# Turning the distance factors on VectorE and through memory, and a new order of joins, masks and gathers, in a graph layer on one core

## What is computed

```python
h  = relu(bn1(conv1(x)));  x_conv = relu(bn2(conv2_17taps(h)) + x)
s  = x @ w_se.T + b_se                    # three numbers for each node
dist = sq[:, None] + sq[None, :] - 2 * s @ s.T
A  = exp(-dist) * mask
x_nmp = A @ relu(x @ w_msg.T + b_msg)
gi = [x_conv, x_nmp] @ w_ih.T + b_ih;  gh = x @ w_hh.T + b_hh
r, z = sigmoid(gi_r + gh_r), sigmoid(gi_z + gh_z)
out = x0 + (1 - z) * tanh(gi_n + r * gh_n) + z * x
```

## Time and profile before

| | us |
|---|---|
| median of 3 runs (287.84 to 287.97) | 287.91 |
| the profiled execution | 288.4 |
| its span | 286.5 |
| TensorE busy (matmuls) | 276.6 (97%) |
| VectorE busy | 243.0 (85%) |
| ScalarE busy | 164.5 (57%) |
| GpSimd busy | 62.5 (22%) |

### The profile page before, as it was taken

The page is one execution under the profiler, slowest core; times in us unless marked ns, Lnnn a source line. Parts: engine busy times, 40 slices in busy tenths (PEclk is TensorE's granted clock), DMA queues, the critical chain, the costliest instruction groups (busy, mean ns, idle before and its releaser), DMA issues.

```text
span 286.5 us, 5279 instructions
## 1 busy us (share of the span) xinstructions
PE 276.6 (97%) x1866; PEld 249.3 (87%) x1866; DVE 243.0 (85%) x551; ACT 164.5 (57%) x271; POOL 62.5 (22%) x124
## 2 busy tenths in 40 slices
PE   7899899999999999999999999999999999999993
PEld 6598886999888998899889998899988998899993
DVE  5998988978998889968998789969998787976565
ACT  3786468745565277545665267564674366561363
POOL 6500020831116102430026102340026100250000
PEclk9999999999999999999999999999999999999999
DMA  7600044566252512654153532645021540023002
GB/s 236 251 3 0 0 150 146 151 182 184 75 174 72 128 70 74 222 68 155 42 176 86 86 130 74 220 47 176 2 84 65 76 146 3 0 37 39 0 2 73
DMA packets 9373, 27.99 MB, mean 98 GB/s; under 512 B 2706, under 2 KB 3220, under 8 KB 8468
## 3 DMA queue, kind: packets, MB, share of 16 engines
q1 hardware_dynamic: 7184, 23.98, 24.0%
q0 software_dynamic: 2016, 3.67, 9.5%
q10 hardware_dynamic: 148, 0.01, 0.0%
HBM read 23.41 MB, written 7.91 MB: 109 GB/s over the span
## 4 chain that ended last, share of the span: by engine, by line
PE 67%; DVE 17%; issue 6%; ACT 5%; POOL 2%; DMA 1%; SPq 0%; DVEq 0%; ACTq 0%; POOLq 0%
PE ps L1194 20%; PE ps L1196 19%; PE ps L1195 19%; PE ps L1278 4%; PE ps L1244 3%; DVE stats L754 2%; DVE wt_lo L796 2%; DMA xin<-x_first 1%; ACT wt_hi L455 1%; POOL rstd L378 1%; PE ps L1255 1%; DVE aff L952 1%; DVE v_lo L877 1%; DVE y L897 1%; PE ps L1268 1%
## 5 line engine op out<-in xcount | busy, mean ns | idle before, releaser
L1194 PE MATMUL ps<-v_hi,wt_hi 128*128 128x256 f32 x320 | 92.6, 289 | 2.6 <-DVE v_lo L865 1.4
L1196 PE MATMUL ps<-v_hi,wt_lo 128*128 128x256 f32 x320 | 90.1, 282 | 0.0
L1195 PE MATMUL ps<-v_lo,wt_hi 128*128 128x256 f32 x320 | 89.9, 281 | 0.0
L1194 PEld LDWEIGHTS ps<-v_hi,wt_hi 128*128 128x128 f32 x320 | 60.3, 188 | 4.7 <-DVE wt_lo L796 1.8
L1195 PEld LDWEIGHTS ps<-v_lo,wt_hi 128*128 128x128 f32 x320 | 60.3, 188 | 0.3
L1196 PEld LDWEIGHTS ps<-v_hi,wt_lo 128*128 128x128 f32 x320 | 60.2, 188 | 0.0
L384 POOL TENSOR_TENSOR scale<-vpe,neg_half 128x8 f32<-128x8 f32 x6 | 10.6, 1768 | 87.8 <-DVE scale L771 87.8
L1194 PE MATMUL ps<-h_hi,wt_hi 128*128 128x512 f32 (+1 forms) x67 | 26.2, 391 | 0.2 <-ACT gate L612 0.2
L1196 PE MATMUL ps<-h_hi,wt_lo 128*128 128x512 f32 (+1 forms) x67 | 25.8, 386 | 0.0
L1195 PE MATMUL ps<-h_lo,wt_hi 128*128 128x512 f32 (+1 forms) x67 | 25.7, 383 | 0.0
L607 ACT ACTIVATE gate<-ps,par 128x512 f32<-128x512 f32 x14 | 9.6, 687 | 20.6 <-PE ps L1196 20.6
(11 more groups left out here) (160 smaller groups left out, 621.5 us busy)
## 6 DMA issues: line engine op xcount, KB each, us to landing
w<-ln_rows SPq DMA_DIRECT2D x6, 1024.0 KB, 4.7
mask<-adj_t SPq DMA_DIRECT2D x8, 512.0 KB, 3.5
out<-x_t SPq DMA_DIRECT2D x7, 512.0 KB, 5.1
out<-gate POOLq DMA_DIRECT2D x14, 256.0 KB, 4.1
xin<-x_nm SPq DMA_DIRECT2D x6, 512.0 KB, 3.3
xt<-x_t SPq DMA_DIRECT2D x6, 512.0 KB, 5.7
w<-w_conv SPq DMA_DIRECT2D x1, 576.0 KB, 5.9
gate<-w_gate SPq DMA_DIRECT2D x1, 576.0 KB, 6.9
```

Source lines behind the costliest of these rows:

```text
L1194: pe.matmul(dst, wt_hi[:, blk, :], hi, start=start, stop=False)
L1195: pe.matmul(dst, wt_hi[:, blk, :], lo, start=False, stop=False)
L1196: return pe.matmul(dst, wt_lo[:, blk, :], hi, start=False, stop=stop)
```

## The change

It touches groups 2 to 7 (`g > BY_TRANSPOSE`, with `BY_TRANSPOSE = 1`); groups 0 and 1 stay.

- `factor_transposes` and `factor_rows` go. VectorE makes one `transpose` of 128 by 256 numbers (`turn`) at the head of its group; it works in blocks of 32x32.
- SyncE stores the result with four DMAs (runs of 32 numbers, 128 bytes; 1024 of them in all), waits, and loads it back with two DMAs (480 runs of 512 bytes) into `rows`. This stands at the head of SyncE's group, ahead of the load of `xts`.
- `distance` moves from behind sub-convolution 2 of 9 to behind the seventh; both gathers move to behind the ninth.
- ScalarE: `exponent` moves behind `m_shared(g, 2)` and behind `h_high` and `graphs_of` of the next group; then come `xc_high`, `ghn_rows(g, 0)`, `n_high` twice.
- VectorE: the masks move from ahead of `ln_apply` to behind `add_shared(g, 1)`, ahead of the last joins and `ln_stats`; `n_low` twice moves behind `xc_low`.
- TensorE: in gates 0, the products of `xc` come ahead of those of the messages.

The diff, cut to its core:

```diff
+            def factor_loads(g):
+                done = g - 1 - BY_TRANSPOSE
+                sp.wait_ge(turned_ready, done + 1)
+
+                upto(sp, rows_landed, 32 * done)
+                for i in range(4):
+                    ns = slice(32 * i, 32 * i + 32)
+                    sp.dma_start(slot_rows.rearrange("(i s) q n -> s q i n", s=SLOT)[:, :, :, ns],
+                                 turned[ns].bitcast(F32).rearrange("s (q i) n -> s q i n", q=2)).then_inc(turned_stored, 16)
+                sp.wait_ge(turned_stored, 64 * (done + 1))
+
+                sp.wait_ge(dist_ps, g)
+                sp.dma_start(rows[:, 0:4:2, :].bitcast(F32), slot_rows).then_inc(rows_landed, 16)
+                sp.dma_start(rows[0:P - KD, 1:4:2, :].bitcast(F32), slot_rows[KD:P]).then_inc(rows_landed, 16)
...
+                if g > BY_TRANSPOSE:
+                    factor_loads(g)
...
                 else:
-                    factor_rows(g)
-                    m_shared(g, 0)
...
+                    m_shared(g, 1)
+                    if ahead:
+                        h_high(g + 1, 0)
+                        h_high(g + 1, 1)
+                        graphs_of(g + 1, 0)
+                        graphs_of(g + 1, 1)
+                    m_shared(g, 2)
+                    exponent(g)
+                if g > BY_TRANSPOSE:
+                    xc_high(g)
+                    ghn_rows(g, 0)
+                    n_high(g, 0, 5)
+                    n_high(g, 1, 7)
...
+            def turn(g):
+                done = g - 1 - BY_TRANSPOSE
+                dve.wait_ge(slots_ready, g + 1)
+
+                upto(dve, turned_stored, 64 * done)
+                dve.transpose(turned[:].bitcast(F32).rearrange("p b (k s) -> p b k s", k=2),
+                              slots[:, :, :, 0:KD].bitcast(F32).rearrange("p k b s -> p b k s")).then_inc(turned_ready, 1)
...
+                    turn(g)
                     update(g - 1, 1)
                     join_b(g, 0)
                     join_b(g, 1)
                     add_h(g)
-                masked(g, 0)
-                masked(g, 1)
...
+                else:
+                    if ahead:
+                        h_low(g + 1, 1)
+                    add_shared(g, 1)
+                    masked(g, 0)
+                    masked(g, 1)
+                    join_y(g, 1, 0)
+                    join_y(g, 1, 1)
+                    if g + 2 < NG:
+                        ln_stats(g + 2)
                 xc_low(g, 0)
                 xc_low(g, 1)
+                if g > BY_TRANSPOSE:
+                    n_low(g, 0, 5)
+                    n_low(g, 1, 7)
...
             def gates_xc(g, c):
                 xc = (xc_hi[:, cols(c)], xc_lo[:, cols(c)])
                 pe.wait_ge(xc_lo_ready, NCH * g + c + 1)
+                if n_last(g, c):
+                    three(bank(4), IH(R, 0), *xc, False, False)
+
+                    pe.wait_ge(n_lo_ready, NCH * g + 1)
+                    three(bank(5), IH(N, 0), *xc, True, False)
+                    three(bank(6), IH(Z, 0), *xc, False, False)
+                    return
...
                 sub_conv(g, 0)
-                if g > 1:
-                    factor_transposes(g)
                 sub_conv(g, 1)
-                if g > 1:
-                    distance(g)
                 sub_conv(g, 2)
...
                 sub_conv(g, 6)
-                gather(g, 1, 7)
+                if g <= BY_TRANSPOSE:
+                    gather(g, 1, 7)
+                else:
+                    distance(g)
                 sub_conv(g, 7)
                 sub_conv(g, 8)
+                if g > BY_TRANSPOSE:
+                    gather(g, 0, 5)
+                    gather(g, 1, 7)
                 gates_h(g, 0, ahead)
                 if ahead:
                     conv1(g + 1, 0, 0)
                     conv1(g + 1, 1, 7)
-                gates_n(g, 0)
-                gates_xc(g, 0)
+                if g <= BY_TRANSPOSE:
+                    gates_n(g, 0)
+                    gates_xc(g, 0)
+                else:
+                    gates_xc(g, 0)
+                    gates_n(g, 0)
```

More of the change, by code:

```diff
@@ L58, with gnn_kernel @@
 NPAR = 14
-def gnn_kernel(nc, x_first, x_nm, x_t, adj_t, w_in, w_conv, w_gate, par_in, row_in, bias_in, ln_rows, out):
+def gnn_kernel(nc, x_first, x_nm, x_t, adj_t, w_in, w_conv, w_gate, par_in, row_in, bias_in, ln_rows, slot_rows, out):
     ctx = ExitStack()
@@ L115, in gnn_kernel @@
         slots = sb("slots", [P, 2, GB, SLOT], F32R)
+        turned = sb("turned", [P, GB, SLOT], F32R)
         rows = sb("rows", [P, 4, P], F32R)
@@ L179, in gnn_kernel @@
             sem("rows_ready"))
+        turned_ready, turned_stored, rows_landed = sem("turned_ready"), sem("turned_stored"), sem("rows_landed")
         dist_ps, e_ready, a_ready, nmp_ps, n_hi_ready, n_lo_ready = (
@@ L190, in gnn_kernel @@
             sem("zd_ready"), sem("out_ready"))
+        BY_TRANSPOSE = 1
         BY_MATMUL = 1
@@ L249, in distances @@
             engine.wait_ge(s_ready, 2 * g + 2)
-            upto(engine, rows_ps, g)
+            if g <= BY_TRANSPOSE + 1:
+                upto(engine, rows_ps, g)
+            else:
+                engine.wait_ge(turned_ready, g - 1 - BY_TRANSPOSE)
             left, right = slots[:, 0], slots[:, 1]
@@ L704, in _ @@
                 candidate(g - 1, 1)
-                if g == 1:
-                    m_shared(g, 0)
+                m_shared(g, 0)
+                if g <= BY_TRANSPOSE:
                     factor_rows(g)
-                else:
-                    factor_rows(g)
[L710 to L723, removed]
+                    exponent(g)
[9 more added lines that the diff above has]
+                    n_high(g, 1, 7)
+                else:
+                    m_shared(g, 1)
+                    if ahead:
+                        h_high(g + 1, 0)
+                        h_high(g + 1, 1)
+                        graphs_of(g + 1, 0)
+                        graphs_of(g + 1, 1)
+                    m_shared(g, 2)
+                    exponent(g)
+                if g > BY_TRANSPOSE:
+                    xc_high(g)
+                    ghn_rows(g, 0)
+                    n_high(g, 0, 5)
+                    n_high(g, 1, 7)
+                else:
+                    ghn_rows(g, 0)
+                    xc_high(g)
                 if ahead:
@@ L1142, in _ @@
                 join_y(g, 0, 1)
-                n_low(g, 0, 5)
+                if g <= BY_TRANSPOSE:
+                    n_low(g, 0, 5)
                 if ahead:
                     h_low(g + 1, 0)
[L1146 to L1153, removed]
+                if g <= BY_TRANSPOSE:
+                    add_shared(g, 1)
+                    n_low(g, 1, 7)
+                    join_y(g, 1, 0)
+                    if ahead:
+                        h_low(g + 1, 1)
[3 more added lines that the diff above has]
+                else:
+                    if ahead:
+                        h_low(g + 1, 1)
+                    add_shared(g, 1)
+                    masked(g, 0)
+                    masked(g, 1)
+                    join_y(g, 1, 0)
+                    join_y(g, 1, 1)
+                    if g + 2 < NG:
+                        ln_stats(g + 2)
                 xc_low(g, 0)
                 xc_low(g, 1)
+                if g > BY_TRANSPOSE:
+                    n_low(g, 0, 5)
+                    n_low(g, 1, 7)
                 if g + 2 < NG:
@@ L1258, in distance @@
             def distance(g):
-                pe.wait_ge(rows_ready, g + 1)
+                if g <= BY_TRANSPOSE:
+                    pe.wait_ge(rows_ready, g + 1)
+                else:
+                    pe.wait_ge(rows_landed, 32 * (g - BY_TRANSPOSE))
                 if g == 0:
@@ L1327, in gates_h, with n_last @@
                 three(bank(6), HH(Z), *h, True, False)
+            def n_last(g, c):
+                return c == 0 and g > BY_TRANSPOSE
             def gates_n(g, c):
+                last = n_last(g, c)
                 nm = [n[:, c * HALF:(c + 1) * HALF, :] for n in (n_hi, n_lo)]
@@ L1334, in gates_n @@
                         pe.wait_ge(wt_lo_ready, LOT_OF_GATES)
+                if last:
+                    three(bank(4), IH(R, 1), *nm, False, True).then_inc(r_ps, 1)
+                    three(bank(5), IH(N, 1), *nm, False, True).then_inc(gin_ps, 1)
+                    three(bank(6), IH(Z, 1), *nm, False, True).then_inc(z_ps, 1)
+                    return
                 three(bank(4), IH(R, 1), *nm, False, False)
@@ L1444, in _ @@
                 sub_conv(g, 5)
-                gather(g, 0, 5)
+                if g <= BY_TRANSPOSE:
+                    gather(g, 0, 5)
                 sub_conv(g, 6)
-                gather(g, 1, 7)
+                if g <= BY_TRANSPOSE:
+                    gather(g, 1, 7)
+                else:
+                    distance(g)
                 sub_conv(g, 7)
                 sub_conv(g, 8)
+                if g > BY_TRANSPOSE:
```

(5 more changed lines are left out.)

## The result

| | before | after |
|---|---|---|
| median of 6 runs, us | 287.94 (287.84 to 288.01) | 289.93 (289.48 to 292.64) |
| ratio to before | | 1.0083 (95%: 1.0065 to 1.0102) |
| the profiled execution, us | 288.4 | 289.6 |
| its span, us | 286.5 | 287.7 |

The kernel became 0.8% slower; 288.5 had been forecast, 0.2% slower (0.58 us, where the medians differ by 1.99). Before, six runs lie within 0.2 us; after, they spread over 3.2. So there are two things to find: what holds the fastest runs 1.64 us above the fastest of before (289.48 against 287.84), and what adds up to 3 us to others.

A forecast was written before the change was run, and what follows sets the result against it. TensorE's own work was taken to bound the kernel. Savings of 3.12 and 0.55 against waits of 4.10 and 0.15 gave +0.58 us: 287.91 + 0.58 = 288.5 us, range 286.9 to 290.8.

The forecast's parts named there:

- the wait at the second half of convolution 1: TensorE waits for n_low before writing bank 7: 0.77 us in groups 2 to 6, 0.25 more in group 2; 4.10 together.
- two chains: Ahead of n_low: ScalarE's list with ghn_rows before n_high, and VectorE's own work, free at G + 2.1; either alone holds it.
- G: Start of the first matmul of gates_h(g, 0), forecast at T + 16.5; convolution 1's second half due at G + 2.79.
- the rivals: TensorE never waits, 284.2 us, chance 0.09; rows late, 294.5 if 1 us late, 0.07; masks late, 290, 0.12.
- What TensorE saves: TensorE's list in groups 2 to 7: transposes 0.44 and one return less 0.08, 0.52 us a group, 3.12 in all.
- one break less: TensorE's gathers put together make one return less, saving 0.08 us a group in groups 2 to 7.
- The wait for the slots: In group 2, TensorE's slot transposes wait for GpSimd's last write of the slots; removing them saves another 0.55 us.
- Group 7: No convolution 1 there; a wait for n_low(0) behind the third matmul of gates_xc costs 0.15 us.
- The way through memory: Turned slots stored and reloaded by SyncE: rows at T + 7.0 to T + 11.9, hidden with 3 us to spare.
- T: The start of group 4, at 154.05, from which the prediction counts; TensorE asks for the rows at T + 11.4.
- The rival of late rows: At distance behind sub-convolution 7, TensorE waits for rows in each of six groups; 1 us late gives 294.5; chance 0.07.
- The turn: VectorE's transpose at the group's head: 0.48 us, hidden in 0.79 us of idle time; nothing taken for groups 3 to 7.

The follow-up runs named there:

- e1: Only ScalarE's list changed against the kernel after: n_high(0) ahead of xc_high, n_high(1) and then ghn_rows behind it; 289.06 us.
- e2: Only VectorE's list changed against the kernel after: the statistics moved behind n_low, no longer ahead of xc_low; 293.11 us.
- e3: Both lists changed against the kernel after: ScalarE n_high(0), xc_high, n_high(1), ghn_rows; VectorE n_low(0), xc_low twice, n_low(1), statistics; 286.2 us.
- e4: The kernel after's order, but slots turned by TensorE and copied by ScalarE as in the kernel before, nothing through memory; 292.57 us.
- e8: e7 with GpSimd's wait of e6 for the landed rows; 284.99 us, ratio to the kernel before 0.9894.
- e9: e4 with the ScalarE and VectorE lists of e3 and the last Z products as in e7; 287.88 us, ratio to before 0.9998.
- e5: The kernel after once more, unchanged, beside later runs on the same chip; 290.74 us.
- e6: The kernel after, with GpSimd issuing the two accumulating output transfers in groups 2 to 7 only when the rows have landed; 289.41 us.
- e7: e3 with the last products of gates 0 in group 7 ordered R, Z, N for R, N, Z; 286.57 us.

## Why the prediction was right, and where it was off

The direction, the range and the mechanism held: the wait at the second half of convolution 1 for `n_low`, five times, with two chains that both hold it (e1, e2, e3). VectorE's own chain came out to 0.1 us: free at G + 2.03 in group 4 where G + 2.1 was forecast. In group 6 only ScalarE's chain holds, since VectorE has no statistics there; I had noted that for group 7 alone. The size did not hold: 0.58 us were forecast, and it was 1.64 between the lowest runs and 1.99 between the medians. The median of 289.93 lies above the 289.5 at which the forecast itself ended, and inside the range only because the rivals had widened it; that much is luck. Point by point.

**What TensorE saves.** Forecast 0.52 a group. From the group's start to the second half of convolution 1 there were 19.78 us (173.83 less 154.05); after, it is due at 173.37, 19.36 from 154.01: 0.42. The transposes' 0.44 is there (e4 against after: 0.43). The 0.08 for one break less is not. Before G the saving is 0.51, as forecast; but the two gathers together take 1.71 us (168.78 to 170.49) where apart they took 0.82 and 0.81, and the one return left falls onto a gate matmul (0.31 at 170.49 for 0.23), behind G, where I had left G + 2.79 as it was. Two gathers and their returns cost 1.79 before and 1.80 after: putting them together saves nothing. Six groups, 0.6 us mis-sized.

**The wait.** Forecast 0.77, measured 0.74 and 0.08, 0.82. `n_low` was done at G + 3.48 (173.97), 0.09 later than forecast, and the handover to TensorE took 0.14 us (the matmul starts at 174.11), not 0.04; the due time, later by the 0.08 above, took most of one of these back. Group 2 was to wait 0.25 more and waits no longer than the others: the list of waits has 2.9 us in five, none over 0.6. The wait for the slots there was worth 0.4 and not 0.55 (e8 against e9), since group 2 without any wait still takes 0.16 more than the next (32.48 for 32.32 in e8). With the terms above these errors nearly cancel: group 2 was forecast 0.05 shorter and is 0.02 shorter.

**Group 7.** Forecast 0.15. The wait for `n_low(0)` is there (272.82 for 272.76, and 0.34 to the next for 0.23, 0.17 in all). The wait for the update gate is missing from the prediction. The step that failed here is my reading of the change's last lines: I noted that `xc` comes first and overlooked that group 7 had its own order of Z ahead of N. From group 7's start on, after is 0.11 longer (34.29 to 34.18; before, group 7 began at 252.31 and the span ended at 286.49), where 0.37 less was forecast.

**The sum.** Groups 3 to 6 gave +1.53, group 2 -0.02, the end +0.11: 1.62 us, the difference of the lowest runs (1.64). Forecast were +1.00, -0.05 and -0.37. The profiled execution of before has 0.41 us more ahead of group 2 (88.00 for 87.59); most runs of before beside the experiments seem to lack that, with spans of 286.0 to 286.2 for its 286.5. So the two profiled executions differ by 1.2 only.

**The way through memory.** Forecast: issues of 0.45, a landing of 1.6 and of 1.7 us and one more for traffic, rows at T + 8. Measured in group 4: 0.66, 2.3 from the start of the last issue, 0.6 and 3.0, rows at T + 9.5. This was inside my bounds (T + 7.0 to 11.9), but the spare time is 1.9 us, not 3. The rival of late rows, which I gave 0.07, is true in one group of many runs, beside the forecast mechanism. I had written it as a thing that happens in all six groups or in none; it happens where the last store falls behind GpSimd's second transfer, and a few tenths of a us decide that. What lifts the median to 289.93 and one run to 292.64 is put down to it from e5 and e6; the only profile of after is of a run without it. The fixed cost of 2.0 us that the Trainium skill gives in DMA: Bandwidth & Descriptors, Anatomy of one DMA, is given there for GpSimd's path; SyncE's stores of 32 KB took the same alone (e6, 2.0), and 3.1 beside the output transfers.

**The turn.** 0.48 forecast, 0.45 measured, hidden as said: the 0.79 us of idle time became 0.24.

## What to carry to other kernels

Where one engine is full, a new order can cost more than the removed operation gives. List for each moved operation who waits for it and how long before it is due, and price the first wait that has no cover left: here 2.9 us of cover for `n_low` became a wait. If two chains meet there, mending one gives a part or nothing (e1 1.1 us, e2 none, e3 4.3); change both lists. A way through memory needs its slack counted against the traffic of the other queues at that moment, and the order in which the transfers are issued counts more than their mean time. A wait that puts this traffic behind it (e6) showed no cost here and was worth 1.3 us.

## What the runs showed of the hardware

A wait of TensorE can cost more than its length. Windows of e3_both in group 5: TensorE was busy without a gap ahead of its wait of 2.14 us for the rows, which ended at 198.33, and busy again behind it. The granted clock, 1.00 until then, falls between 199 and 200 to 0.50, the 1.2 GHz level, and is back at the other, 2.4 GHz, from 203 on:

```profile
198.30:199.00 0.70, 0.67 (x10) 0.60 (x11) 0.00 (x0) 0.18 (x1) 0.00 (x0) 1.00 0.35 140
199.00:200.00 1.00, 1.00 (x9) 1.00 (x8) 0.12 (x1) 0.85 (x1) 0.00 (x0) 0.85 0.00 0
200.00:201.00 1.00, 1.00 (x7) 1.00 (x6) 1.00 (x2) 0.00 (x0) 0.00 (x0) 0.50 0.00 0
...
203.00:204.00 1.00, 1.00 (x11) 1.00 (x10) 0.48 (x1) 0.00 (x0) 0.00 (x0) 0.95 1.57 639
```

At 0.50 the matmuls of 256 columns follow each other in 0.21 us for 0.12. The group lost 3.73 us to a wait of 2.14. The same is seen in e1 (wait 2.16, group 5 36.44 us for 32.95 in group 4) and e2 (2.56; 37.28 for 33.14), with some 3 us at 0.50 each. In e5_after_again a wait of 0.97 cost 1.04, and in e7 one of 1.25 cost 1.32, both with the clock at 1.00 in the window of the group. The five waits of 0.6 for `n_low` leave the clock at 1.00 too (the windows of after).

VectorE's 32x32 block transpose of 128x256 numbers in float32 took 0.45 us, no more than other work of that size (the join, 0.48). Issuing one of the four stores, 256 runs of 128 bytes, cost SyncE 0.66 us, where I had taken 0.45; the issue of a load of `xts` takes 0.42 to 0.43 in the kernel before.
